# One product for two tiles and one sum for four in the edge scores of layer 0

## The reference

```python
k_rel = jnp.einsum('nhd,rhde->rnhe', k, rel_att)
key_e = k_rel[edge_type, edge_src]
val_e = v_rel[edge_type, edge_src]
att = (q[edge_dst] * key_e).sum(-1) * rel_pri[edge_type] / jnp.sqrt(jnp.float32(dk))
...   # softmax of att over the edges of one destination and relation, then the weighted sum of val_e
```

## Time and profile before

| | |
|---|---|
| median of three executions | 4846.09 us (4845.42 to 4862.79) |
| span of the profiled execution, first to last instruction | 4441.9 us |
| busy in the span | PE 2583.6, DVE 2897.9, ACT 1649.6, POOL 2232.5 us |
| first and last gather of `edge_scores` start at | 568.19 and 1673.44 us |
| last score copied to the table | 1679.85 us |

### The profile page before, as it was taken

The page is one execution under the profiler, slowest core; times in us unless marked ns, Lnnn a source line. Parts: engine busy times, 40 slices in busy tenths (PEclk is TensorE's granted clock), DMA queues, the critical chain, the costliest instruction groups (busy, mean ns, idle before and its releaser), DMA issues. The chain is left out here.

```text
span 4441.9 us, 56033 instructions
## 1 busy us (share of the span) xinstructions
PE 2583.6 (58%) x10078; PEld 1680.6 (38%) x10079; DVE 2897.9 (65%) x5983; ACT 1649.6 (37%) x4237; POOL 2232.5 (50%) x2263
## 2 busy tenths in 40 slices
PE   0499856766666661000388886666356565666653
PEld 0255433434333330000266663443244444444432
DVE  4544445555555556999788886766366566666657
ACT  2244333333333332321166664343233434343443
POOL 4322267777777770000144442221677777777751
PEclk9999978778777775555699998997677777676776
DMA  6366699999999993000377771000666666666652
GB/s 203 121 259 264 258 318 310 315 310 316 313 314 311 315 312 97 0 0 0 116 229 230 228 230 57 18 17 18 154 189 187 193 187 193 186 190 189 190 150 88
DMA packets 577883, 841.19 MB, mean 189 GB/s; under 512 B 137539, under 2 KB 472271, under 8 KB 570917
## 3 DMA queue, kind: packets, MB, share of 16 engines
q0 software_dynamic: 128272, 451.36, 31.9%
q1 hardware_dynamic: 443056, 382.08, 27.5%
q10 hardware_dynamic: 6430, 6.43, 0.5%
HBM read 549.59 MB, written 291.24 MB: 189 GB/s over the span
## 5 line engine op out<-in xcount | busy, mean ns | idle before, releaser
L1911 POOL DMA_INDIRECT g_rows<-x1t,srci x880 | 854.4, 971 | 286.8 <-issue 254.7
L991 POOL DMA_INDIRECT rows<-kv,kvi x880 | 838.3, 953 | 286.7 <-issue 244.4
L1037 PE MATMUL psD<-qs,hot 128*128 x1760 | 698.1, 523 | 257.5 <-DVE prod L1078 202.6
L1078 DVE TENSOR_TENSOR prod<-rows,psD 128x256 f32<-128x256 f32 x880 | 363.9, 418 | 482.7 <-DMA rows<-kv,kvi 375.5
L2065 PE MATMUL g_psM<-g_rows,g_hot 128*128 128x264 f32 x1760 | 572.4, 480 | 76.3 <-DVE g_rows L2183 69.4
L1329 POOL TENSOR_TENSOR wv<-vrows,wgt 128x1024 f32<-128x1024 f32 x110 | 209.8, 1907 | 779.2 <-DVE vhot L1447 778.4
L1037 PEld LDWEIGHTS psD<-qs,hot 128*128 128x128 f32 x1760 | 381.1, 251 | 524.8 <-issue 306.8
L1424 PE MATMUL psM<-wv,vhot 128*128 128x260 f32 x1760 | 431.2, 394 | 77.8 <-DVE run L1443 65.0
L1057 ACT ACTIVATE off<-psB,npiota 128x256 f32<-128x256 f32 x440 | 207.3, 471 | 688.0 <-PE psB L1028 685.6
L2065 PEld LDWEIGHTS g_psM<-g_rows,g_hot 128*128 128x128 f32 x1760 | 391.0, 234 | 170.5 <-issue 92.9
L1424 PEld LDWEIGHTS psM<-wv,vhot 128*128 128x128 f32 x1760 | 323.0, 191 | 185.9 <-DVE run L1443 138.0
(11 more groups left out here) (412 smaller groups left out, 4373.4 us busy)
## 6 DMA issues: line engine op xcount, KB each, us to landing
val_v<-rows SPq DMA_DIRECT2D x220, 512.0 KB, 5.0
vrows<-val_v SPq DMA_DIRECT2D x220, 512.0 KB
sums_v<-g_run SPq DMA_DIRECT2D x110, 528.0 KB, 3.7
g_drow<-drow_v SPq DMA_DIRECT2D x55, 512.0 KB
rows<-kv,kvi POOLq DMA_INDIRECT x880, 5.3
g_rows<-x1t,srci POOLq DMA_INDIRECT x880
g_ndt<-nodeb SPq DMA_DIRECT2D x440, 6.0 KB
hs<-hsort SPq DMA_DIRECT2D x51, 130.0 KB, 2.1
```

The costliest lines, as they stand in the source:

```text
L991: nc.gpsimd.indirect_dma_start(out=rows[:, k], out_offset=None, in_=table, in_offset=bass.IndirectOffsetOnAxis(ap=index[:, i * SLOTS + k:i ...
L1037: nc.tensor.matmul(psD[:, k % 4, 0:cols], hot[:, t % 2, j * P:(j + 1) * P], node[:, ds(blk[t], 1)].rearrange("p o d -> p (o d)"), start=Tr ...
L1078: ins = nc.vector.tensor_tensor(prod[:, k % 4], rows[:, k, 0:D], psD[:, k % 4, 0:D], ALU.mult)
L1911: nc.gpsimd.indirect_dma_start(out=rows[:, i % NBUF, k, 0:ROW1], out_offset=None, in_=dr["x1t"], in_offset=bass.IndirectOffsetOnAxis(ap=v[ ...
```

## The change

A visit becomes the unit of product, of PSUM bank and of semaphores, and a group of four tiles the unit of the sums:

- Both matmuls of a visit write to one bank of `psD` (columns 0 to 255 and 256 to 511), which four visits use by turns. TensorE waits once per visit, and adds 1 to `dst_done` once per visit.
- VectorE multiplies a visit's two tiles in one instruction of 512 columns (`product`), after it has waited for both gathers.
- `sums` reduces a group's 1024 columns to 16 numbers in one instruction, and writes them into `att`. It follows the product of the next group's first visit in VectorE's order, except at the end of a turn, where it stands behind the turn's last product.
- `used` goes up by 4 ahead of `sums`, once the group's two products are done; so for the first three groups of a turn it stands behind the product of the next group's first visit.
- `sc` and the copy per turn are gone. `prod` holds two groups of four tiles (it held four tiles). The branches for layer 1 in this function are cut.

```diff
-        prod = sb("prod", [P, 4, D])
-        sc = sb("sc", [P, SLOTS, H])
+        prod = sb("prod", [P, 2, GS, D])
...
-                pe.sem_inc(dst_done, 4)
+                pe.sem_inc(dst_done, 2)
...
                         pe.wait_ge(hot_done, i * (SLOTS // 2) + t + 1)
+                        pe.wait_ge(prod_done, i * (SLOTS // 2) + t + 1)
                         for j in range(2):
-                            k = 2 * t + j
-                            pe.wait_ge(prod_done, i * SLOTS + k + 1)
-                            nc.tensor.matmul(psD[:, k % 4, 0:cols], hot[:, t % 2, j * P:(j + 1) * P],
-                                             node[:, ds(blk[t], 1)].rearrange("p o d -> p (o d)"), start=True, stop=True).then_inc(dst_done, 1)
+                            ins = nc.tensor.matmul(psD[:, t % 4, j * D:(j + 1) * D], hot[:, t % 2, j * P:(j + 1) * P],
+                                                   node[:, ds(blk[t], 1)].rearrange("p o d -> p (o d)"), start=True, stop=True)
+                        ins.then_inc(dst_done, 1)
...
-                        act.wait_ge(dst_done, 2 * V)
+                        act.wait_ge(dst_done, V + 1)
...
-                    for k in range(SLOTS):
-                        dve.wait_ge(got[k], 16 * (i + 1))
-                        dve.wait_ge(dst_done, K + k + 5)
-                        if L == 0:
-                            dve.wait_ge(sc_done, K + k + 1)
-                            ins = nc.vector.tensor_tensor(prod[:, k % 4], rows[:, k, 0:D], psD[:, k % 4, 0:D], ALU.mult)
-                            ins.then_inc(prod_done, 1)
-                            if k:
-                                reduce_(k - 1)
...
-                    dve.wait_ge(sc_done, K + SLOTS + 4)
-                    nc.vector.tensor_copy(att[:, :, ts(i, SLOTS)], sc[:].rearrange("p k h -> p h k")).then_inc(sc_kept, 1)
-                    dve.wait_ge(sc_kept, i + 1)
+                    def product(t):
+                        for k in (2 * t, 2 * t + 1):
+                            dve.wait_ge(got[k], 16 * (i + 1))
+                        dve.wait_ge(dst_done, i * (SLOTS // 2) + t + 3)
+                        dve.wait_ge(sc_done, i * (SLOTS // GS) + t // 2 + 1)
+                        nc.vector.tensor_tensor(prod[:, t // 2 % 2, t % 2 * 2:t % 2 * 2 + 2], rows[:, 2 * t:2 * t + 2, 0:D],
+                                                psD[:, t % 4].rearrange("p (j d) -> p j d", j=2), ALU.mult).then_inc(prod_done, 1)
+
+                    def sums(g):
+                        dve.wait_ge(prod_done, i * (SLOTS // 2) + 2 * g + 6)
+                        dve.sem_inc(used, GS)
+                        nc.vector.tensor_reduce(att[:, :, ts(i * (SLOTS // GS) + g, GS)].rearrange("p h t -> p t h"),
+                                                prod[:, g % 2].rearrange("p t (h d) -> p t h d", h=H), AX.X, ALU.add).then_inc(sc_done, 1)
+                    for t in range(SLOTS // 2):
+                        product(t)
+                        if t and t % 2 == 0:
+                            sums(t // 2 - 1)
+                    sums(SLOTS // GS - 1)
+                dve.wait_ge(sc_done, NC // GS + 2)
+                dve.sem_inc(sc_kept, NI)
```

## The result

The changed kernel takes 4919.34 us (median of four, 4915.70 to 4935.17), the kernel before in the same comparison 4851.75; the ratio is 1.0147, interval 1.0124 to 1.0170. That is 68 us slower. I had forecast 4846.7 us, in a range of 4839 to 4864, and no change, so the prediction was wrong.

The account below looks back on a forecast made before the run. POOL's gathers, one per 1.257 us, were taken to bound the edge scores; VectorE's savings and the later release counted nothing, the tail +0.6 us: 4846.09 + 0.6 = 4846.7 us, range 4839 to 4864.

Parts of the forecast that it names:

- What bounds the kernel: Edge-score stage: POOL issues one gather per 1.257 us throughout; no wait for VectorE, TensorE or a store lengthens a step.
- The 404.2 us around the span: Time outside the profiled span of 4441.9 us, beside runs of 4846.09 us; carried over unchanged into the forecast.
- So the later release costs nothing: POOL's wait for freed slots in the edge scores: the release comes later but still in time, so 0 us added.
- The margins, 10.6 us before and 7.8 after: Time to spare between release of slots and the gather reusing them; 5.8 us at the slowest landing, 3.9 in first turn.
- The rival of the late release: Release ahead of a group's first gather stalls POOL: 54 us over 54 later turns, 4900 us; 5 in 100.
- The argument against it: Against late-release stalls: longest landings eat 2 us of 7.8, and products at a turn's start wait less for TensorE.
- VectorE's and TensorE's parts: Edge scores: VectorE's work falls 155 us, counted as nothing beside the gathers; TensorE keeps its matmuls, shorter mutual waits priced zero.
- The tail: After the last gather: table turning about 7.3 us after its start, where it was 6.7; +0.6 us, bounds +0.4 to +1.0.
- VectorE as the bound: Rival: VectorE and TensorE waits pace the gathers, so 155 us come off, 4691 us; 3 in 100.
- That copies held POOL: Rival: each of 55 copies kept POOL from work 0.22 us; removing them saves 12 us, 4834.7 us; 5 in 100.
- a clash in the gathers' length: Gather beside a 0.22 us copy took 0.96 us like its neighbours, so removing the copies was counted as freeing nothing.

Follow-up runs that it names:

- the second trace: The kernel before, unchanged, traced again: 4853.16 us, ratio 1.0000, span 4854.4 us.
- 12 ahead: Changed kernel with early release, GpSimd at most 12 tiles ahead instead of 16: 4456.55 us (0.9998), 4450.79 (1.0005), 4866.54 (0.9941) in three sets against the kernel before.

## Why the prediction was wrong

**What bounds the kernel: right for the execution I read, not for those that were timed.** Gathers paced at 1.257 us hold in the first trace and on two chips. On the chip of the holds GpSimd waits some 230 us in this stage before any change.

**The 404.2 us around the span: this is the sentence that failed first.** I carried them over as a constant. Of the runs that have a span beside their time, none has more than 2 us around it. The gap between span and runs was the one sign, ahead of the experiments, that waits were missing from the trace: 1334.0 us from first to last gather in the second trace against 1105.2 makes 229 of them, and the layer 1 stage has most of the rest.

**"So the later release costs nothing": the step whose failure made the 68 us.** The margins, 10.6 us before and 7.8 after, were worked out from landings and instruction lengths without a hold. (The 0.69 us taken off for the product was too much: the release goes out as that product starts, and GpSimd went on at 1020.18, before its end at 1020.47. So 8.5 us and not 7.8; it changes nothing.) With holds both margins are gone: ScalarE starts up to 12.8 us behind its matmul, over 1 us in 173 visits before and 206 after (counted from the end of ScalarE's own instruction before, where that comes later, over 1 us in 114 and 142 visits and up to 11.1). What counts is what the release still stands behind when the hold ends: for the kernel before the product of visit 1, which is ready, for the changed one that of visit 2, which must still pass three engines. The difference of the long steps is 62 us over 55 turns, 1.1 us a turn. The rival of the late release named place and mechanism, with "one stall of 1 us in each of the 54 later turns" as its price, and 4900 us; it had 5 chances in 100. Its 1 us was a round number worked out from nothing, so that it came near is luck. The argument against it, that a product waits for TensorE less than before at the start of a turn, is borne out by the trace without holds (14 waits of 61.7 us in place of 75 of 92.2); with holds it is exactly this wait that opens the loss.

**VectorE's and TensorE's parts: costs right, bookkeeping partly wrong.** Products take 686 ns (forecast 0.69 us) and sums 1216 (1.25). The Trainium skill, "VectorE: DVE Perf Modes", section "The TRN2 errata — SBUF-src ops pay a fixed extra latency per instruction", gives an f32 add of two tiles of N columns as (N+151)/0.96 ns; taken for a product too, that makes an estimate of 691 for 512, and the trace agrees. The same section says that many small tiles pay a fixed cost each and a single large one pays it once; that is true here (two products of 256 columns at 418 ns against one of 512 at 686), and worth nothing in time, since without a hold no gather waits for VectorE. Busy time in the stretch fell from 638.47 to 543.75 us, not to 480: I took instruction lengths, which overlap, from busy time, in which overlap is counted once. Idle time before products grew from 482.7 to 571.6 us, as said; VectorE's waits for TensorE fell from 92.2 (75 times) to 61.7 (14). TensorE's waits for VectorE's products were to fall and rose in total, 200.4 (215 times) to 264.5 (206); without holds no gather waits for them.

**The tail: right.** Last gather to the turning of the table takes 1680.06 - 1672.65 = 7.41 us without holds, forecast 7.3, before 6.7. The whole change there measures +1.4 us, forecast +0.6, both inside the interval.

**The other rivals.** VectorE as the bound did not come: 68 us slower, and no change without holds. That copies held POOL did not either: without them a step is 1.257 us still (1105.3 us over 879 steps). But the two engines do get in each other's way, in the direction that I did not look in. The 55 copies of the kernel before are not all of 0.22 us, and come to 14.4 us and not 12:

```profile
L1094 DVE COPY early<-sc x55: 216/218/416, 594.9 to 1679.8; 128x64 f32 x55
```

```profile
715.36 0.95 POOL L991 DMA_INDIRECT rows<-kv,kvi  x1 [0.30 <-issue]
715.91 0.42 DVE L1094 COPY early<-sc 128x64 f32 x1
```

Twenty of the 55 take 228 ns or more, and 19 of these end 7 to 15 ns behind the end of the gather beside them, as this one does; the gathers beside them take 949 to 956 ns as ever. So the copy waits for the gather, and not the gather for the copy. In the prediction I looked for a clash in the gathers' length alone, where it does not show.

## What to carry to other kernels

Before a trace is used for a sum, set its span beside the times; where hundreds of us lie between, it shows another condition than the one that is timed, and a margin read from it is no margin. A release of buffers belongs right behind the last reader: put behind the next piece of work it cost nothing on the chip without holds where it was run, and 1.1 us a turn where TensorE's increments were late. When work is made coarser, keep its releases where they were: here that meant moving one release, and gave all of the 68 us back.

## What the runs showed of the hardware that was not expected

- The same kernel takes 4847 to 4893 us on one chip and 4448 to 4458 us on two others. In the first case TensorE's increments arrive late, so that ScalarE starts up to 14.8 us behind its matmul in this stage (the kernel with 20 slots), the DMA engines move the same bytes at 258 GB/s (kernel before) in place of 313, and the sum of GpSimd's long steps lies at 223 to 246 us for 16 or 20 slots or 12 ahead. Each of the two fast chips was met in one set of runs only, so that the condition belongs to the chip, and not to the hour, is likely and not shown.
- Of the three engines' increments only TensorE's are late. In all eight traces with holds TensorE starts at most 0.26 us behind ScalarE's matrix and VectorE's product, whichever it waits for last, and in the second trace of the kernel before GpSimd restarts 0.33 us behind VectorE's.
- Two more signs tell the two conditions apart in all sixteen traces. Those with holds record 27,629 to 28,352 updates of semaphores over the whole execution, the others 67,712 to 69,382; and a packet of a gather takes 177 to 178 ns on average (between 568 and 1674 us) against 166 to 167. What either has to do with the holds is not shown.
- A VectorE copy within SBUF can be held to the end of a gather that GpSimd works on: 19 of 55 copies, up to 416 ns in place of 216.
- Writing out five turns of the loop removed none of these holds (55 long steps stay 55).
- What makes and what ends a hold stays open. Both of my theories of it failed. In seven of the eight traces with holds, more than half of those over 3 us end while GpSimd stands in a long step, between the end of one gather and the start of the next (94 of 144 in the second trace of the kernel before, where these pauses are 19% of the stage). That may be cause or effect.
